# Expert attention: both heads' weights turned by transfers, expert sums as one VectorE reduction

## The reference, cut to what matters

```
x = x + expert_attention(layernorm(x))    # 8 heads, 5 experts a head, 64 channels, top 3
  s = sigmoid(x @ Ws);  d = sigmoid(x @ Wd)     # one gate for each token, head and expert
  s, d = the 3 largest of 5 kept, others 0
  q = sum_e d[e] * (x @ Wq[e])                  # for each head, 64 channels
  k = sum_e s[e] * (x @ Wk[e]);  v = sum_e s[e] * (x @ Wv[e])
  p = softmax(q k^T / 8);  o = p v              # 1024 x 1024 weights for each head and batch
  out = sum over heads and experts of kept_d[e] * o @ Wo[e]
```

## Time and profile before

| | |
|---|---|
| median of three runs | 2760.68 us (2760.38 to 2760.92) |
| span of the profiled execution | 2759.2 us; its own time lies some 1.5 us above it, if it ran like the median |
| PE busy | 2441.3 us (88%), 21822 matmuls; weight loads 1594.3 us |
| DVE busy | 2004.9 us (73%) |
| ACT busy | 1517.2 us (55%) |
| POOL busy | 1862.8 us (68%) |
| transfers | queue q1: 37.0% of 16 engines' span |
| scores of the first stage touched | from 1404 us; of the second from 2162 us, to the end |

### The profile page before, as it was taken

One profiled execution on the slowest core, in us unless ns is written; L12 is line 12 of the kernel. 1 busy time (PEld: TensorE's weight loads), 2 busy tenths in 40 slices (PEclk: granted clock), 3 DMA queues, 4 the chain that ended last, 5 costly groups with the idle time before them and its releaser, 6 DMA issues. The chain is left out here.

```text
span 2759.2 us, 57518 instructions
## 1 busy us (share of the span) xinstructions
PE 2441.3 (88%) x21822; PEld 1594.3 (58%) x21822; DVE 2004.9 (73%) x3570; ACT 1517.2 (55%) x2197; POOL 1862.8 (68%) x1738
## 2 busy tenths in 40 slices
PE   6787786886999999999788999999798889999986
PEld 3554544643566666667545666665534456666655
DVE  7999445455777777777588888887386888888872
ACT  4222122332888888888525666666462256665564
POOL 1888100001999999999457899998510578999984
PEclk9999788988999999999899999999898999999998
DMA  1000000002889988899612333333201133333332
GB/s 44 1 1 1 0 23 13 1 23 66 140 154 159 160 149 161 158 152 157 135 20 55 62 62 62 62 62 70 60 13 60 20 55 62 63 62 62 62 70 58
DMA packets 632753, 193.27 MB, mean 70 GB/s; under 512 B 614920, under 2 KB 623624, under 8 KB 632480
## 3 DMA queue, kind: packets, MB, share of 16 engines
q1 hardware_dynamic: 632480, 189.60, 37.0%
HBM read 20.70 MB, written 1.05 MB: 8 GB/s over the span
## 5 line engine op out<-in xcount | busy, mean ns | idle before, releaser
L2307 PE MATMUL banks<-g_w,normed_t 128*128 128x320 f32 x1536 | 494.9, 449 | 28.6 <-DVE g_scratch L2591 28.4
L1778 DVE TENSOR_REDUCE at_negmax<-banks 128x1 f32<-128x1024 f32 x256 | 301.6, 1220 | 153.5 <-PE banks L1690 153.5
L2591 DVE TENSOR_TENSOR g_scratch<-banks,g_gate 128x640 f32<-128x640 f32 x384 | 314.3, 822 | 106.9 <-PE banks L2307 103.4
L1755 POOL TENSOR_TENSOR at_p_lo<-at_p,at_p_hi 128x640 bf16<-128x640 f32 x256 | 356.1, 1408 | 12.8 <-ACT at_p_hi L1743 11.4
L1597 DVE TENSOR_REDUCE g_negmax<-banks 128x1 f32<-128x1024 f32 x256 | 310.8, 1219 | 59.7 <-PE banks L1507 59.4
L2307 PEld LDWEIGHTS banks<-g_w,normed_t 128*128 128x128 f32 x1536 | 263.7, 190 | 121.4 <-DVE g_scratch L2591 48.1
L1561 ACT ACTIVATE g_p<-banks,g_negmax 128x1024 f32<-128x1024 f32 x256 | 285.9, 1117 | 72.1 <-DVE g_negmax L1597 64.3
L1584 POOL TENSOR_TENSOR g_p_lo<-g_p,g_p_hi 128x512 bf16<-128x512 f32 x256 | 301.1, 1197 | 30.2 <-POOL g_z L2514 19.4
L1736 ACT ACTIVATE at_p<-banks,at_negmax 128x1024 f32<-128x1024 f32 x256 | 285.7, 1116 | 6.4 <-DVE at_negmax L1778 6.4
L1574 ACT CAST g_r_hi<-banks 128x512 bf16<-128x512 f32 x128 | 75.0, 586 | 379.1 <-PE banks L1522 379.1
L1690 PE MATMUL banks<-at_k_t,at_q 64*128 64x512 f32 x1024 | 257.7, 622 | 17.9 <-POOL at_k_t L2039 9.1
(11 more groups left out here) (426 smaller groups left out, 6644.2 us busy)
## 6 DMA issues: line engine op xcount, KB each, us to landing
at_swapped<-at_crossed SPq DMA_DIRECT2D x128, 128.0 KB, 2.8
g_w<-in_ex_w SPq DMA_DIRECT2D x2, 2880.0 KB, 11.7
f_w<-in_W SPq DMA_DIRECT2D x2, 1024.0 KB, 5.6
at_rope<-in_rope SPq DMA_DIRECT2D x1, 2048.0 KB, 10.1
at_t_hi<-at_p_hi SPq DMA_TRANSPOSE x128, 3.6
at_t_lo<-at_p_lo SPq DMA_TRANSPOSE x128, 3.6
g_t_hi<-g_p_hi SPq DMA_TRANSPOSE x128, 3.1
g_t_lo<-g_p_lo SPq DMA_TRANSPOSE x128, 3.2
```

Source lines behind the costliest of these rows:

```text
L1755: self.nc.gpsimd.tensor_tensor(self.p_lo[:, j % self.RING, h, :], self.p[:, j % 2, h, 0:self.BY_DMA * P], self.p_hi[:, j % self.RING, h, : ...
L1778: self.nc.vector.tensor_reduce(self.negmax[:, j % 2, h:h + 1], self.core.banks[:, first:first + 2, :], AX.XY, ALU.max, negate=True).then_i ...
L2307: nc.tensor.matmul(out[:, 0:ED], core.xt[:, at:at + P], w[:, kind * H + tile // (T * BATCH) * 2 + h, :], start=True, stop=True).then_inc(p ...
L2591: v.tensor_tensor(qk_product[:, tile % 2, kind] if kind < 2 else v_product[:, tile % 2], core.banks[:, bank:bank + 2, 0:ED].rearrange("p h ...
```

## The change

It does two things in both stages.

First, `HeadStream` has no part that PE turns. `p_hi`, `p_lo` hold all 1024 keys of both heads, ACT and POOL split 128 x 1024 a head, and a transfer turns 128 x 2048 where it turned 128 x 1024. `transpose`, `subtract`, `act_copy`, `act_rest` and `dve_lo` are gone.

Second, the weights lie with the five experts innermost (a reordering of the input on the host; the kernel loads the same bytes), so the gate product is laid out as channel, expert, and the experts are summed by one DVE reduction over five neighbouring elements: for v (128 x 640 to 128) and now also for q and k (128 x 1280 to 256), which POOL did. POOL has no sums left. `o` has 8 places where it had 16, with a wait for a `route` of eight tiles before.

```diff
-        self.p_hi, self.p_lo = (sb(n, [P, 2, 2, CHUNK], BF16) for n in ("p_hi", "p_lo"))
-        self.t_hi, self.t_lo = (sb(n, [P, 2, 2 * self.GROUPS, P], BF16) for n in ("t_hi", "t_lo"))
+        self.p_hi, self.p_lo = (sb(n, [P, 2, self.TURNED * P], BF16) for n in ("p_hi", "p_lo"))
+        self.t_hi, self.t_lo = (sb(n, [P, 2, self.TURNED, P], BF16) for n in ("t_hi", "t_lo"))
...
     def values(self, pe, j, h):
         b = j // self.T % 2
         self.wait_turned(pe, j)
-        self.wait_split(pe, j, h)
...
-            n, block = self.GROUPS * h + k, slice((k - self.GROUPS) * P, (k - self.GROUPS + 1) * P)
-            if k < self.GROUPS:
-                hi, lo = self.t_hi[:, j % 2, n], self.t_lo[:, j % 2, n]
-            else:
-                hi, lo = (self.r_hi[:, j % 2, block], self.r_lo[:, j % 2, block]) if h == self.BY_PE else (self.u_hi[:, j % 2, block], self.u_lo[:, j % 2, block])
+            hi, lo = self.t_hi[:, j % 2, self.T * h + k], self.t_lo[:, j % 2, self.T * h + k]
...
-        self.nc.scalar.copy(self.p_hi[:, j % 2, h, :], self.p[:, j % 2, h, 0:CHUNK]).then_inc(self.hi_ready, 1)
+        self.nc.scalar.copy(self.part(self.p_hi, j, h), self.p[:, j % 2, h]).then_inc(self.hi_ready, 1)
...
-        self.nc.gpsimd.tensor_tensor(self.p_lo[:, j % 2, h, :], self.p[:, j % 2, h, 0:CHUNK], self.p_hi[:, j % 2, h, :],
+        self.nc.gpsimd.tensor_tensor(self.part(self.p_lo, j, h), self.p[:, j % 2, h], self.part(self.p_hi, j, h),
                                      ALU.subtract).then_inc(self.lo_ready, 1)
...
-        sp.dma_start(dst[:, j % 2], src[:, j % 2].rearrange("p h n -> p (h n)"), transpose=True).then_inc(self.turned[j % 2], 16)
+        sp.dma_start(dst[:, j % 2], src[:, j % 2], transpose=True).then_inc(self.turned[j % 2], 16)
...
-                hs.transpose(pe, j, 0)
...
-                hs.subtract(pe, j)
...
-                hs.transpose(pe, j, 1)
...
             for j in range(STEPS):
                 unit, t = j // T, j % T
                 for h in range(2):
                     hs.pool_lo(pool, j, h)
-                if j + LEAD - 1 < TOTAL:
-                    sum_tile(j + LEAD - 1)
                 if j:
                     route(j - 1)
...
                 v.tensor_tensor(qk_product[:, tile % 2, kind] if kind < 2 else v_product[:, tile % 2],
-                                core.banks[:, bank:bank + 2, 0:ED].rearrange("p h (e c) -> p h e c", c=D),
-                                gate[:, tile // (T * BATCH), 1 if kind == 0 else 0, row:row + 2, :].unsqueeze(3).to_broadcast([P, 2, E, D]),
+                                core.banks[:, bank:bank + 2, 0:ED].rearrange("p h (c e) -> p h c e", e=E),
+                                gate[:, tile // (T * BATCH), 1 if kind == 0 else 0, row:row + 2, :].unsqueeze(2).to_broadcast([P, 2, D, E]),
                                 ALU.mult).then_inc(product_ready, 1)
...
-                v.tensor_reduce(hs.v[:, tile % T, :, 0:D], v_product[:, tile % 2].rearrange("p h e c -> p h c e"), AX.X,
-                                ALU.add).then_inc(v_ready, 1)
...
+                v.tensor_reduce(hs.v[:, tile % T, :, 0:D], v_product[:, tile % 2], AX.X, ALU.add).then_inc(v_ready, 1)
+
+            def sum_tile(tile):
+                unit, t = tile // T, tile % T
+                if t in (0, 4) and unit:
+                    dve.wait_ge(qk_full, unit * 4 - 2 + t // 2)
                 dve.wait_ge(product_ready, (last_of(tile, False) + 1) // 2)
...
+                v.tensor_reduce(tok[:, :, t].rearrange("p k h c -> p k (h c)"),
+                                qk_product[:, tile % 2].rearrange("p k h c e -> p k (h c) e"), AX.X, ALU.add).then_inc(tok_ready, 1)
...
-                hs.dve_lo(dve, j)
                 beside(2)
                 if j:
-                    hs.dve_normalise(dve, j - 1)
+                    hs.dve_normalise(dve, j - 1, z_ready)
+                if j + LEAD < TOTAL:
+                    sum_tile(j + LEAD)
```

More of the change, by code:

```diff
@@ L1510, in scores @@
                     ins.then_inc(self.s_full, 1)
[L1512 to L1531, removed]
     def values(self, pe, j, h):
@@ L1598, in dve_max, with dve_normalise @@
                                      negate=True).then_inc(self.max_ready, 1)
[L1600 to L1605, removed]
+    def dve_normalise(self, dve, j, routed):
         dve.wait_ge(self.av_done, 2 * j + 2)
@@ L2187, in expert_attention_stage @@
         z_t = sb("z_t", [P, 3, P])
-        hs = HeadStream(core, ctx, tag, home=lambda j, h: 6 if h and j >= TOTAL - T else 4, sums=5)
+        hs = HeadStream(core, ctx, tag, sums=5)
         STEPS = UNITS * T
@@ L2206, in expert_attention_stage @@
         early_bank = lambda n: core.ps[n % 4 if n < 4 * T else 4 + n % 4]
[L2208 to L2220, removed]
-            eng.wait_ge(tok_ready, sums_before(tile, False))
-            if sums_before(tile, True):
-                eng.wait_ge(tok_early, sums_before(tile, True))
         def first(j):
@@ L2310, in turn @@
             def turn(unit, m, out):
-                wait_tok(pe, unit * T + 4 * (m // 2 + 1))
+                pe.wait_ge(tok_ready, unit * T + 4 * (m // 2 + 1))
                 for t in range(4):
@@ L2462, in _ @@
                     place_out(k)
-                hs.act_rest(act, j)
                 if not last:
@@ L2466, in _ @@
                 if t == 0 and unit:
-                    hs.act_split_values(act, unit, (v_ready, (unit + 1) * T - T // 2))
+                    hs.act_split_values(act, unit, (v_ready, (unit + 1) * T))
                 if not last:
                     hs.act_exp(act, j + 1, 1)
-                hs.act_copy(act, j, 1)
-                if not last:
                     hs.act_hi(act, j + 1, 1)
@@ L2506, in route @@
                     pool.wait_ge(mask_ready, j // T + 1)
-                step(g.tensor_tensor(routed[:], hs.o[:, unit % BATCH, t].unsqueeze(2).to_broadcast([P, 2, E, D]),
+                step(g.tensor_tensor(routed[:], hs.o[:, t].unsqueeze(2).to_broadcast([P, 2, E, D]),
                                      mask[:, unit // BATCH, 1, 2 * tile:2 * tile + 2, :].unsqueeze(3).to_broadcast([P, 2, E, D]), ALU.mult))
@@ L2625, in _ @@
             keep((0,), range(T))
-            for n in range(4 * T):
-                if n % 2 == 0:
-                    apply_gates(n, n % 4)
-                if n % 4 == 3 and n // 4 in DVE_SUMS:
-                    sum_early(n // 4)
+            for tile in range(T):
+                apply_gates(4 * tile, 0)
+                if tile:
+                    sum_tile(tile - 1)
+                apply_gates(4 * tile + 2, 2)
+            sum_tile(T - 1)
             dve.wait_ge(gates_ready, CHUNKS)
@@ L2635, in _ @@
                 hs.dve_max(dve, 0, h)
-            for n in range(4 * T, EARLY):
-                if n % 2 == 0:
-                    apply_gates(n, 4 + n % 4)
-                if n < 6 * T and n % 4 == 3:
-                    sum_values(n // 2 - 2 * T)
-            hs.dve_split_values(dve, 0)
+            for tile in range(T):
+                n = 4 * T + 2 * tile
+                apply_gates(n, 4 + n % 4)
+                if tile:
+                    sum_values(tile - 1)
+            sum_values(T - 1)
+            for tile in range(T, LEAD):
+                n = 6 * T + 4 * (tile - T)
+                apply_gates(n, 4)
+                if tile > T:
+                    sum_tile(tile - 1)
+                else:
+                    hs.dve_split_values(dve, 0)
+                apply_gates(n + 2, 6)
+            sum_tile(LEAD - 1)
             for j in range(STEPS):
@@ L3302 @@
     half = wkv.shape[1] // 2
-    give("ex_w", _np.stack([_np.asarray(inputs["L1_ffn_Wq"]), wkv[:, :half], wkv[:, half:]]))
+    inner = lambda a: _np.asarray(a).reshape(P, 8, 5, 64).transpose(0, 1, 3, 2).reshape(P, -1)
+    give("ex_w", _np.stack([inner(a) for a in (inputs["L1_ffn_Wq"], wkv[:, :half], wkv[:, half:])]))
     give("ex_gate", _np.concatenate([_np.asarray(inputs["L1_ffn_Ws"]), _np.asarray(inputs["L1_ffn_Wd"])], axis=1))
```

89 lines of the change are left out of this document (19 added, 70 removed).

## The result

The changed kernel takes 2911.78 us (median of four runs, 2904.47 to 2914.12), the kernel before 2760.80 beside it: ratio 1.0537, 95% interval 1.0519 to 1.0554. I had forecast slower, 2846, with 2785 to 2895 as range. The direction holds, the size doesn't: +151 instead of +85.

The account below looks back on a forecast made before the run. The loop through low parts, transfer, values, o and route was to set 9.2 us a step; terms summed to +42.7 us a stage, +85 for two, so 2846 us against 2760.68, with 2785 to 2895 as the 8-in-10 range.

Parts of the forecast that it names:

- Loop 2: Low parts, their transfer, values, o, route, low parts two tiles on: 18.0 us for two steps, 9.2 a step with additions.
- Loop 1: Exchange of PE and DVE through banks 6 and 7, gate products and projections: 8.45 us a step, as today.
- Steps 16 to 52: Main stretch of a stage: 37 steps at 9.2 us, 340.4 against 316.3, +24.
- values to route: Piece of the low-parts loop, from values of head 0 through projections and o to route: 5.66 us.
- The last steps keep their pace: End of a stage, behind steps 53 to 59: no change in time per step.
- Steps 53 to 59, +3: Late steps, 55.0 us before: 7.6 for three without projections, 8.8 for four; +3 a stage.
- Steps 0 to 5, +7: First steps, bound by DVE choosing experts: the sums on DVE add 1.13 us each, +7 a stage.
- 6 to 15, +2: Ten steps with one addition less in route in the first two units: 87.4 against 85.2 us, +2 a stage.
- the end, +3.3: End of a stage: the last low parts (1.9) and their transfer (1.4) stand bare, +3.3.
- Before step 0, +3.4: Stretch of 16 gate products and first sums before the steps: sums of v +0.5, of q and k +2.7; together +3.4.
- A: Rival: the longer transfer's added half moves in 0.7 us, 8.85 a step; 2813 us, or 2785 if quicker. Chance 0.18.
- B: Rival: data waits for a doubled issue's end (2902 us) or reductions stay at the slower rate (2912). Chance 0.12.
- C: Rival: faster than before, POOL's 7.6 us sets the step; about 2702 us. Chance 0.05.

Follow-up runs that it names:

- route_late: The changed kernel with route of o one step later on GpSimd (behind the low parts of the next tile), up to the last unit: 2821.78 us, ratio 1.0216.
- by_head: The changed kernel with each transfer cut in two (one a head, 128x1024), values, copies and low parts waiting for their own head alone: 2821.24 us, ratio 1.0212.
- p2_sums_only: The kernel before with only the reordered weights and all sums on VectorE; TensorE still turns half, transfers stay 128x1024: 2794.75 us, ratio 1.0121.
- filler: The changed kernel with four more matmuls (128x512, constants, unused bank) on TensorE ahead of the values of head 0 in every step: 2873.89 us, ratio 1.0408.
- best_fill: The changed kernel with transfers by head, later route, early sums divided, q and k sums around gate product b2, four 128x512 matmuls in the last five steps: 2734.61 us.
- late_head: The changed kernel with both transfers cut by head and route one step later: 2811.74 us, ratio 1.0181.
- early_pool: The changed kernel with sums ahead of the steps and in steps 0 to 4 divided between GpSimd and VectorE, later ones on VectorE in halves: 2872.00 us, ratio 1.0398.
- one part: The kernel before with only the transfers changed (128x2048, no weight turned on TensorE), sums of q and k still on GpSimd: 2969.87 us, ratio 1.0757.

## Why the prediction was wrong, by its steps

- **Loop 2 as the bound, and its prices**: right. Landing, route, low parts and reductions are within 0.2 us, three kinds of run put transfer and route in it, and with full clock a step takes 9.14 (steps 16 to 23).
- **Loop 1 at 8.45**: 8.57 to 8.64 where no transfer holds PE and the clock is at 1.00 (route_late, by_head); 0.15 short. (p2_sums_only has 8.62 too, but there PE is nearly full.)
- **Steps 16 to 52, "37 x 9.2 = 340.4"**: this is the term that failed: 354.9 in the second stage, 358.4 in the first, so +39 and +42, not +24. At full clock the price holds (9.28 a step over 13 passes); with a stretch of the lower clock it is 9.77. The step in it was "values to route ... 5.66", added up from matmuls at full clock; behind a wait of 2 us it was 6.91. I had written that PE "then waits for the transfer" and counted the wait as worth nothing. It costs: the clock falls at its end in most cases, and filling it gave 9.9 us back. The Trainium skill, "TensorE: Matmul & The Clock Gate", section "HAM oscillation — how this bites in real kernels", describes waits for transfers that put PE back to half clock. The trace agrees in kind (2.30 against 1.32 us), though the waits in the Trainium skill's example are some 3 to 5 us long, while here the clock fell behind one of 2.09. I had not weighed it.
- **"The last steps keep their pace (8.9)"**: wrong, 10.68 at clock 0.82. The scores take 2.81 us there instead of 1.99; with filler (second fence) 1.99 and a pace of 8.90, and in best_fill the pace is 8.9 again.

```profile
2848.51 2.81 PE L1490 MATMUL banks<-g_k_t,g_q 64*128 64x512 f32 x8
```
```profile
2809.18 1.99 PE L1490 MATMUL banks<-g_k_t,g_q 64*128 64x512 f32 x8
```

- **Steps 53 to 59, +3**: +6.5 at clock 0.85 (+8.5 at 0.82 in the first stage). The cause stays open: route_late and by_head have 60.3 and 60.6, both together 55.8 at 0.94 in the second stage but 59.1 at 0.87 in the first; filler doesn't help (62.9).
- **Steps 0 to 5, +7; 6 to 15, +2; the end, +3.3**: 7.0, 1.3 and 3.6 in the second stage (5.6, 4.6 and 4.3 in the first). Right in size. But "bound by DVE" does not fix the time of steps 0 to 5 alone: kernels with the same DVE work there (changed, route_late, by_head, late_head) took from 65.0 us at clock 0.95 to 71.5 at 0.83, and the kernel before had 0.97. Part of the 7 may be the clock (no run shows how much), and then the hit is in part luck. **Before step 0, +3.4**: 5.7 (0.9 before the first scores, 4.8 behind them), 6.9 in the first, where I had 3.4; p2_sums_only has the 4.8 and early_pool doesn't, so it comes with the sums on DVE.
- A stage: forecast +42.7, measured 74.7 and 66.2, and 2.4 ahead of the first. Of the surplus of 32 and 23.5, steps 16 to 52 hold 18 and 14.5, steps 53 to 61 hold 8 and 7; of the rest the stretch before step 0 holds 3.5 and 2.3.
- **The rivals.** A's rate is refuted: 128x1024 lands in 3.2 (p2_sums_only), 128x2048 in 4.5, so the added half costs 1.3 us, not 0.7; against the 350 to 400 GB/s that the Trainium skill gives ("Advanced Engine Details and Errata", "X-Bar Transpose (TRN2)"), this is some 200 (256 KB in 1.3 us). B hit the size (2902, 2912) by chance: the landing of 4.5 us and reductions of 0.81 and 1.48 us show neither a held-back landing nor slow reductions. C's condition, loop 2 out of the way, is met in late_head, and it is still loop 1 at 8.57 and not POOL's 7.6 that sets the step.

## What to carry to other kernels

When a change makes a wait on TensorE longer, price the matmuls behind it at the lower clock too, above all if they lie in the loop that makes the wait: here the clock's share of steps 16 to 52 was 10 to 11 us a stage, by the filler's run, beside 24 foreseen. A loop that runs through a late consumer (route, between two writes of the low parts) can be opened by order alone: putting it one tile later gave back 90 of 151 us here. Take apart what a change bundles: one part cost 209 us alone, and with the other, which costs 33 alone, both cost 151.

## What I had not expected of the hardware

- The clock falls behind waits of 2.1 us, but not behind each: the four matmuls of a projection took 2.30 us behind one of 2.09, and 1.32 behind one of 2.08 us 19 us later. Four matmuls of 128x512 in the wait kept it at 1.00 (rounded) over 345 us; four of 128x16 gave 0.97.
- A transposing transfer of 128x2048 bf16 occupies SyncE's queue 1.85 us in the median for the low parts and 2.72 for the high parts, at most 4.2 (1.23 for low parts of 128x1024), and the landing of the low parts grows by 1.3 only.
